# A gather in steps of 8 slots from a table written by runs, and expert outputs gated by matmuls with diagonal gates

## The reference, cut to what matters

```
h = x @ W_gat                                   # 4096 nodes x (4 heads x 4 experts)
a_src, a_dst = (h*att_src).sum, (h*att_dst).sum # one number for a node and head
e = leaky_relu(a_src[src] + a_dst[dst], 0.2)    # for 524288 edges and each node's loop
alpha = softmax of e over the edges of one dst
agg = segment_sum(h[src] * alpha, dst) + b_gat
scores = layernorm(agg, gamma, beta).mean over heads      # 4096 x 4 experts
top 2 of the 4 scores, w = softmax of these two, 0 for the other two
out = sum over experts of w[e] * (gelu(x @ W1[e] + b1[e]) @ W2[e] + b2[e])
```

## Time and profile before

| | |
|---|---|
| median of 3 runs | 1105.31 us (1095.95 to 1108.36) |
| the profiled execution | 1085.32 us |
| its span, first to last instruction | 1083.6 us |
| mean granted clock of TensorE | 0.852 of full |
| busy: PE, DVE, ACT, POOL | 765.5, 661.9, 349.7, 204.3 us |
| last normalisation ends, features begin | about 806 us |
| first and last indirect DMA issued | 845.3 and 972.7 us |
| gates known, first gate transposition | 1025.6 us |
| last addition of outputs ends | 1075.6 us |

### The profile page before, as it was taken

The page is one execution under the profiler, slowest core; times in us unless marked ns, Lnnn a source line. Parts: engine busy times, 40 slices in busy tenths (PEclk is TensorE's granted clock), DMA queues, the critical chain, the costliest instruction groups (busy, mean ns, idle before and its releaser), DMA issues.

```text
span 1083.6 us, 13898 instructions
## 1 busy us (share of the span) xinstructions
PE 765.5 (71%) x4268; PEld 467.3 (43%) x4308; DVE 661.9 (61%) x1367; ACT 349.7 (32%) x519; POOL 204.3 (19%) x200
## 2 busy tenths in 40 slices
PE   4369920108989989989987787899489999203753
PEld 1212210107878878878842332544155433002332
DVE  3599778755656646646658677594663233226754
ACT  4421130004544535545532333510024566103500
POOL 5180010000000000000040000100000677770055
PEclk9588965558999999999999899999787999655866
DMA  8000000010000000000000000000017000110001
GB/s 304 0 1 1 1 0 0 2 77 3 2 1 0 0 0 0 0 0 0 0 1 1 0 0 0 2 1 1 2 42 15 8 8 7 8 8 2 1 20 58
DMA packets 19866, 15.60 MB, mean 14 GB/s; under 512 B 14016, under 2 KB 17728, under 8 KB 19440
## 3 DMA queue, kind: packets, MB, share of 16 engines
q1 hardware_dynamic: 16512, 13.93, 5.2%
q0 software_dynamic: 3312, 1.16, 1.6%
HBM read 10.43 MB, written 4.65 MB: 14 GB/s over the span
## 4 chain that ended last, share of the span: by engine, by line
DVE 16%; PE 15%; issue 10%; POOL 8%; DMA 3%; DVEq 1%; ACT 1%; POOLq 0%; PEld 0%; PEldq 0%; SPq 0%
PE banks L1516 12%; POOL rows_g L576 7%; DVE kept L1208 2%; DVE wide_buf L1168 1%; DMA rows_g<-table_d,g_idx 1%; PE banks L1881 1%; PE banks L1797 1%; DVE wide_buf L1174 1%; POOL wide_buf L592 1%; DVE tie L1172 1%; DVE kept L1267 1%; DMA table_d<-shared 1%; DVE T L846 1%; DVE round_k L1266 1%; PE banks L1549 1%
## 5 line engine op out<-in xcount | busy, mean ns | idle before, releaser
L1117 DVE TENSOR_TENSOR wide_buf<-banks,small 128x1024 f32<-128x1024 f32 x72 | 88.1, 1224 | 118.3 <-ACT small L713 118.3
L1516 PE MATMUL banks<-wide_buf 128*128 128x256 f32 (+1 forms) x720 | 145.7, 350 | 0.0
L1516 PEld LDWEIGHTS banks<-wide_buf 128*128 128x128 f32 x720 | 123.1, 195 | 12.9
L576 POOL DMA_INDIRECT rows_g<-table_d,g_idx x96 | 99.4, 1035 | 125.8 <-DVEq L1426 96.9
L1516 PE MATMUL banks<-XP 128*128 128x32 bf16 (+1 forms) x1168 | 95.2, 222 | 27.4 <-DVE XP L971 27.4
L1516 PE MATMUL banks<-taps_w,small 128*128 128x128 f32 x618 | 92.2, 296 | 20.5 <-issue 20.5
L1516 PEld LDWEIGHTS banks<-taps_w,small 128*128 128x128 f32 x618 | 85.2, 202 | 30.9 <-issue 21.1
L711 ACT ACTIVATE small<-banks,neg_x 128x512 f32<-128x512 f32 x72 | 49.5, 688 | 151.6 <-remote 64.7
L1516 PEld LDWEIGHTS banks<-XP 128*128 128x128 bf16 (+1 forms) x1168 | 60.1, 107 | 61.7 <-issue 32.4
L727 ACT COPY wide_buf<-banks 128x512 f32<-128x512 f32 (+1 forms) x87 | 49.6, 570 | 95.8 <-PE banks L1516 95.1
L971 DVE TENSOR_TENSOR XP<-lo_b,XP 128x2048 bf16<-128x2048 bf16 x64 | 77.8, 1215 | 0.0
(11 more groups left out here) (314 smaller groups left out, 1168.1 us busy)
## 6 DMA issues: line engine op xcount, KB each, us to landing
wide_buf<-in_edges SPq DMA_DIRECT2D x2, 1536.0 KB, 15.3
generic_d<-generic SPq DMA_DIRECT2D x1, 2064.0 KB, 7.3
X<-in_x SPq DMA_DIRECT2D x4, 512.0 KB, 5.0
out_x<-X SPq DMA_DIRECT2D x4, 512.0 KB, 2.6
rows_g<-table_d,g_idx POOLq DMA_INDIRECT x96, 2.4
wide_buf<-in_edges SPq DMA_DIRECT2D x2, 512.0 KB, 9.8
XP<-in_m_w SPq DMA_DIRECT2D x2, 512.0 KB, 4.5
taps_w<-in_w_dcn SPq DMA_DIRECT2D x1, 576.0 KB, 16.7
```

The lines of the kernel that those rows point to most:

```text
L576: pool.indirect_dma_start(rows_g[:, half, k, :], None, table_d, bass.IndirectOffsetOnAxis(ap=g_idx[:, c:c + 1], axis=0)).then_inc(rows_lan ...
L1117: nc.vector.tensor_tensor(near_w[s % RING], banks[:, 0:2, :], hat_x[:, h:h + 1, :].to_broadcast([P, 2, CHUNK]), ALU.mult).then_inc(w_done, 1)
L1516: return nc.tensor.matmul(o, l, r, start=start, stop=stop, **kw)
```

## The change

The change has three parts.

The gather runs in steps of 8 slots (`STEP`), two halves of 4, and so many steps as the fullest partition needs (`N_STEPS`, from the same counts). The one-hot work of a step stands between the waits for its two halves, it is half as large, and it reads `bucket_dst` without the copy `per_hi`. POOL is released right behind the computation of a_dst, and the large comparison of `slot_keys` becomes `slot_ends`, called after L1421. `table_d` is written with each partition's 32 rows as one run ("(p t) f"), and the slots' indices are computed to match, in two more instructions.

The scoring chain is shortened: gamma and beta are folded into `gat_g` and `gat_b` ahead of time, and gamma's product and the sum over heads stand ahead of the wait for the square root.

The experts' outputs become pixel-major: `expert_out` takes the hidden values as the stationary operand, 128 pixels at a time, 8 matmuls of 128 columns in place of 2 of 512, and ACT only copies. Gating is done by PE: for each chunk one matmul of 512 columns adds the gated biases (`m_b2` tiled over the partitions, times `gate_rows`, which POOL makes from the transposed gates), and 16 matmuls of 128 columns multiply a block of `y_exp` with a diagonal matrix of one expert's gates for 128 pixels, all summed in one bank. DVE makes 12 diagonals of a chunk in one instruction of 128x1536, ACT the other 4. DVE adds the bank to X.

```diff
-            sp.dma_start(table_d.rearrange("(t p) f -> p t f", p=P), table[:, :, :]).then_inc(table_out, 16)
+            sp.dma_start(table_d.rearrange("(p t) f -> p t f", p=P), table[:, :, :]).then_inc(table_out, 16)
             sp.wait_ge(adst_ready, 1)
-            sp.dma_start(table_d_dst.rearrange("(t p) h -> p t h", p=P), a_dst[:, :, :]).then_inc(adst_out, 16)
+            sp.dma_start(table_d_dst.rearrange("(t p) h -> p t h", p=P), a_dst[:, :, :]).then_inc(adst_in, 16)
...
+            nc.gpsimd.memset(own_tiles[:, :], 1.0).then_inc(sel_made, 1)
+            for base, step in ((0, -EXPERTS), (EXPERTS - 1, EXPERTS)):
+                pool.wait_ge(sel_made, 11 if base == 0 else 12)
+                nc.gpsimd.affine_select(out=own_tiles[:, :], in_=own_tiles[:, :], compare_op=ALU.is_ge, fill=0.0, base=base,
+                                        pattern=[[step, HIS]], channel_multiplier=1 if base == 0 else -1).then_inc(sel_made, 1)
...
-                    for k in range(HALFR):
-                        c = half * HALFR + k
-                        pool.indirect_dma_start(rows_g[:, half, k, :], None, table_d,
-                                                bass.IndirectOffsetOnAxis(ap=g_idx[:, c:c + 1], axis=0)).then_inc(rows_landed[half][k // GROUP], 16)
-
-            with pool.Fori(0, ways) as r:
+                    for k in range(HALF_STEP):
+                        c = half * HALF_STEP + k
+                        pool.indirect_dma_start(rows_step[:, half, k, :], None, table_d,
+                                                bass.IndirectOffsetOnAxis(ap=g_idx[:, c:c + 1], axis=0)).then_inc(rows_landed[half][k // 2], 16)
+
+            with pool.Fori(0, steps) as r:
...
-            with pool.Fori(0, CHUNKS) as i:
-                pool.wait_ge(gated, EXPERTS * (i + 1) + 2)
-                pool.sem_inc(passed, 1)
-                for e in (0, 2):
-                    nc.gpsimd.tensor_tensor(y_exp[e][:, bass.ds(i, 1), :], y_exp[e][:, bass.ds(i, 1), :],
-                                            y_exp[e + 1][:, bass.ds(i, 1), :], ALU.add).then_inc(gated_b, 1)
-                pool.wait_ge(gated_b, 3 * i + 2)
-                pool.sem_inc(passed, 1)
-                nc.gpsimd.tensor_tensor(y_exp[0][:, bass.ds(i, 1), :], y_exp[0][:, bass.ds(i, 1), :],
-                                        y_exp[2][:, bass.ds(i, 1), :], ALU.add).then_inc(gated_b, 1)
+            pool.wait_ge(gates_known, 3)
+            pool.wait_ge(sel_made, 13)
+            for i in range(CHUNKS):
+                if i >= 2:
+                    pool.wait_ge(gated, i - 1)
+                nc.gpsimd.tensor_tensor(gate_rows[i % 2], gate_t.unsqueeze(1).to_broadcast([P, CHUNK // P, P]),
+                                        own_tiles[:, 4 * i:4 * i + 4].unsqueeze(2).to_broadcast([P, CHUNK // P, P]), ALU.mult).then_inc(rows_gated, 1)
...
-                nc.scalar.activation(y_exp[e][:, i, :], ps[4 + e % 2][:, :], ACT.Identity, bias=m_b2[:, e:e + 1]).then_inc(my_done, 1)
+                nc.scalar.copy(y_exp[e][:, i, :], ps[4 + e % 2][:, :]).then_inc(my_done, 1)
...
+            act.wait_ge(gates_known, 2)
+            nc.scalar.copy(gate_t, ps[0][:, 0:P]).then_inc(gates_known, 1)
+            for i in range(CHUNKS):
+                if i >= 2:
+                    act.wait_ge(gated, i - 1)
+                for e in range(EXPERTS):
+                    last = nc.scalar.activation(gate_diag[i % 2][:, 3, e, :], ident[:, :], ACT.Copy, scale=gate[:, 4 * i + 3, e:e + 1])
+                last.then_inc(diag_act, 1)
...
+                steps_ = num[:, N_STEPS:N_STEPS + 1]
+                run(nc.vector.tensor_scalar(steps_, counts_max[:, 0:1], float(STEP - 1), None, ALU.add))
+                run(nc.vector.tensor_scalar(steps_, steps_, 3, None, ALU.logical_shift_right))
...
-                step(nc.vector.tensor_scalar(slot_idx[:, 0:P], slot_int, LAST, None, ALU.bitwise_and))
+                step(nc.vector.tensor_scalar(slot_lo, slot_int, P - 1, 5, ALU.bitwise_and, ALU.logical_shift_left))
+                step(nc.vector.tensor_scalar(slot_idx[:, 0:P], slot_int, 7, HIS - 1, ALU.arith_shift_right, ALU.bitwise_and))
+                step(nc.vector.tensor_tensor(slot_idx[:, 0:P], slot_idx[:, 0:P], slot_lo, ALU.add))
...
+            def slot_step(R, r):
+
+                g = R * STEPS + r
+                step, n = chained(m1_chain, g * SLOT_STEP, True)
+
+                def rows_in(half):
+                    at = r * STEP + half * HALF_STEP
                     for landed in rows_landed[half]:
-                        dve.wait_ge(landed, g * (16 * GROUP) + 16 * GROUP)
+                        dve.wait_ge(landed, g * (16 * 2) + 16 * 2)
                         dve.sem_inc(passed, 1)
-                    step(nc.vector.tensor_copy(g_idx[:, half * HALFR:(half + 1) * HALFR], slot_idx[:, bass.ds(at + ROUND, HALFR)]))
+                    step(nc.vector.tensor_copy(g_idx[:, half * HALF_STEP:(half + 1) * HALF_STEP], slot_idx[:, bass.ds(at + STEP, HALF_STEP)]))
                     dve.sem_inc(idx1_ready, 1)
-                    step(nc.vector.tensor_copy(feat_s[:, :, bass.ds(at, HALFR)], rows_g[:, half, :, 0:HE].rearrange("p k f -> p f k")))
-                    step(nc.vector.tensor_tensor(z_by_head[:, :, bass.ds(at, HALFR)], z_by_head[:, :, bass.ds(at, HALFR)],
-                                                 rows_g[:, half, :, HE:ROW].rearrange("p k h -> p h k"), ALU.add))
+                    step(nc.vector.tensor_copy(feat_s[:, :, bass.ds(at, HALF_STEP)], rows_step[:, half, :, 0:HE].rearrange("p k f -> p f k")))
+
+                def logits_in(half):
+                    cols = bass.ds(r * STEP + half * HALF_STEP, HALF_STEP)
+                    step(nc.vector.tensor_tensor(z_by_head[:, :, cols], z_by_head[:, :, cols],
+                                                 rows_step[:, half, :, HE:ROW].rearrange("p k h -> p h k"), ALU.add))
                     dve.sem_inc(max1_done, 1)
-                assert n[0] == SLOT_ROUND
+
+                rows_in(0)
+                step(nc.vector.tensor_tensor(oh_slots, his[:, bass.ds(r * STEP, STEP)].unsqueeze(2).to_broadcast([P, STEP, HIS]),
+                                             lane[:, 0:HIS].unsqueeze(1).to_broadcast([P, STEP, HIS]), ALU.is_equal))
+                step(nc.vector.tensor_tensor(pick_grid, oh_slots.unsqueeze(2).to_broadcast([P, STEP, HEADS, HIS]),
+                                             bucket_dst[:, :, :].rearrange("p t h -> p h t").unsqueeze(1).to_broadcast([P, STEP, HEADS, HIS]), ALU.mult))
+                step(nc.vector.tensor_reduce(z_by_head[:, :, bass.ds(r * STEP, STEP)].rearrange("p h k -> p k h"), pick_grid, AX_X, ALU.add))
+                logits_in(0)
+                rows_in(1)
+                logits_in(1)
+                assert n[0] == SLOT_STEP
...
+            dve.sem_inc(max1_done, 2)
...
-            dve.wait_ge(adst_in, 16)
-            run(nc.vector.tensor_copy(per_hi[:, :, :], bucket_dst[:, :, :].rearrange("p t h -> p h t")))
-            dve.sem_inc(max1_done, 2)
-            ways = dve.value_load(num[0:1, N_WAYS:N_WAYS + 1], min_val=1, max_val=WAYS)
+            slot_ends()
+            dve.wait_ge(adst_in, 32)
+            steps = dve.value_load(num[0:1, N_STEPS:N_STEPS + 1], min_val=1, max_val=STEPS)
             rest = dve.value_load(num[0:1, N_REST:N_REST + 1], min_val=0, max_val=MAX_ROUNDS // WAYS - 1)
-            with dve.Fori(0, ways) as r:
-                slot_round(0, r)
+            with dve.Fori(0, steps) as r:
+                slot_step(0, r)
...
-            run(nc.vector.tensor_scalar(stat[:, 0, :], stat[:, 0, :], 1.0 / HE, None, ALU.mult))
-            run(nc.vector.tensor_tensor(prod[:, :, :], prod[:, :, :], wide(0), ALU.subtract))
+            run(nc.vector.scalar_tensor_tensor(prod[:, :, :], wide(0), -1.0 / HE, prod[:, :, :], ALU.mult, ALU.add))
             run(nc.vector.tensor_tensor(agg, prod[:, :, :], prod[:, :, :], ALU.mult))
             run(nc.vector.tensor_reduce(stat[:, 1, :], agg, AX_X, ALU.add))
-            run(nc.vector.tensor_scalar(stat[:, 1, :], stat[:, 1, :], 1.0 / HE, None, ALU.mult))
             dve.sem_inc(f_ask, 1)
+            run(nc.vector.tensor_tensor(prod[:, :, :], prod[:, :, :], gat_g[:, :].unsqueeze(1).to_broadcast([P, HIS, HE]), ALU.mult))
+            run(nc.vector.tensor_reduce(score[:, :, :], prod[:, :, :].rearrange("p t (h e) -> p t e h", h=HEADS), AX_X, ALU.add))
             dve.wait_ge(f_exp, 2)
             run(nc.vector.reciprocal(stat[:, 1, :], stat[:, 1, :]))
-            run(nc.vector.tensor_tensor(prod[:, :, :], prod[:, :, :], wide(1), ALU.mult))
-            run(nc.vector.tensor_tensor(prod[:, :, :], prod[:, :, :], row(1), ALU.mult))
-            run(nc.vector.tensor_tensor(prod[:, :, :], prod[:, :, :], row(2), ALU.add))
-
-            run(nc.vector.tensor_reduce(score[:, :, :], prod[:, :, :].rearrange("p t (h e) -> p t e h", h=HEADS), AX_X, ALU.add))
```

(54 more changed lines are left out.)

94 lines of the change are left out of this document (39 added, 55 removed).

## The result

The changed kernel takes 1071.23 us (median of 4 runs, 1068.46 to 1072.75), the kernel before 1100.63 (4 runs, 1095.3 to 1108.36): ratio 0.9725, 95% interval 0.965 to 0.9799. The forecast was 1079, with a range of 1060 to 1098. The profiled executions show less: spans of 1083.6 and 1071.0 us, so 12.6 us, where the sum gave 26. Later runs of both, beside each other, took that side: 1083.63 against 1071.15. The total was met, and by luck; its parts were not, and this is what the rest is about.

A forecast was written before the change was run, and what follows sets the result against it. Behind the last normalisation it took three stretches to carry the change: the gather's start, its length (POOL's issue sets the pace) and gating. +1.2 - 15 - 11 gave -26 from 1085.3, about 1059; plus 20 for the median, 1079 (range 1060 to 1098).

The forecast's parts named there:

- The total: Whole kernel: 26 us less, about 1059 us for a profiled execution, 1079 us for the median of runs.
- Counts: Counts before the rounds: four more dependent DVE operations on the path to the last normalisation, +1.2 us.
- Start of the gather: Table write 2.5 us, first gather about 825, 20 us earlier; `last_row` lands about 831, DVE takes first rows about 839.3.
- Length of the gather: 88 gathers in 11 steps, 11.3 us a step, set by the handshake; last rows answered at 961.4, -15 us.
- Rival C: The gather gives nothing: 12.5 us instead of 11.3, or 12 steps; +12 to +14 us, 1092; chance 0.13.
- The bound of 10.0 a step: Lower bound for a gather step, by POOL's issue alone: 8 x 1.25 us, giving -28 us.
- The experts: Experts beside the gather: smaller matmuls add 1.7 us for 28 experts, end near 928, covered by the gather.
- Scores: Scoring chain on DVE after the gather: shorter, gates known 2.1 us earlier.
- Gating: Last stage, on PE: 4.4 us a chunk, last addition over at 1064.8 against 1075.58; -11 us including the scoring chain's 2.1.
- rival D: PE pairs run at the low clock through gating: 71 us instead of 35, 1114 us; chance 0.06.
- rival B: POOL's configuration for gating is loaded behind the wait: +7 us, 1086 us; chance 0.17.
- The tail: The store behind the last addition: taken to stay as it was, no gain.

The follow-up runs named there:

- a0_again: The changed kernel, unchanged, run again beside runs of the kernel before on the same chip: 1071.15 us, ratio 0.989.
- a_ends: The changed kernel with only the 4.4 us comparison for the segment ends moved into the wait for the last row: 1066.56 us, ratio 0.9837.
- a_perhi: The changed kernel with the a_dst rows copied once to a contiguous tile, which the one-hot product reads instead of the strided operand: 1063.04 us, ratio 0.9807.
- a_first: The changed kernel with a step's one-hot compare, product and reduce ahead of the wait for its first rows: 1053.27 us, ratio 0.9714.
- a_best: The changed kernel with contiguous operand, one-hot work ahead of the first wait, and the segment-ends comparison in the wait for the last row: 1040.40 us, ratio 0.9602.
- b3_written: The kernel before with POOL's loop of the last stage written out eight times, with constant waits and addresses: 1084.04 us, ratio 1.000.
- b0_again: The kernel before, unchanged, profiled once more: 1086.04 us.
- b1_table: The kernel before with only the table part: table written by runs, indices to match, buffer credits given right after the table: 1070.28 us, ratio 0.9861.
- a_step16: The changed kernel with steps of 16 slots instead of 8, so 96 gathers instead of 88: 1060.22 us, ratio 0.9773.
- b2_gate: The kernel before with the gating part alone: pixel-major expert outputs, diagonal gates, products accumulated in PSUM: 1072.86 us, ratio 0.9892.

## Why the prediction was right in the total and wrong in its parts

- **Counts** (+1.2): features start 1.3 us later (807.73 against 806.40). Right, as far as this can be read: over the kept traces the start lies between 804.54 and 807.88 with the old counts and between 805.75 and 809.43 with the new, so one pair of profiles can't show 1.2 us.
- **Start of the gather**: table write 2.2 us (2.5 forecast), first gather 825.76 (825). `last_row` was forecast to land at 831; DVE goes on at 835.35. I had priced the a_dst write and the read behind it at 6 to 7 us by subtraction, 15.1 less the table's 8.98, as if the two writes had simply added. They had overlapped: without the table's, from the a_dst issue at 824.01 to DVE at 835.35, write and read still take 11.3, and in a0_again that write alone lands after 11.6. This and the 0.4 us more until the loop put DVE's first rows at 843.98 instead of 839.3. a_ends shows that a delay here reaches the end: the 4.4 us moved gave 4.6.
- **Length of the gather**, the step that failed: "the period of a step is ... 11.3 us". It is 12.8. The form was right (3 x 1.25, landing, DVE's work, POOL's answer), and in the step shown above three terms were larger. DVE's work takes 5.44 us against 4.7, by the product alone: 1.98 instead of 1.22 us (I took its length from the contiguous one of the kernel before, and the change drops just that copy; a_perhi gives 0.8 back). POOL's way from release to first gather takes 0.94 us against 0.3. The first half lands 2.66 us behind its last issue (892.47) against 2.5. Together 3.75 + 2.66 + 5.44 + 0.94 = 12.8. The gaps on DVE, 1.1 us, were no larger than the 1.2 forecast. The second step starts 6.0 us late (850.29 against 844.3), the nine steps to the last one take 116.2 us instead of 103.7: 18.5 us, and -15 became +3.4. Rival C came true in size (12.5 in its text), but not for its reason: landing reaches 3.0 to 3.65 us only in the last three steps, and the rest is the product and POOL's answer.
- **The bound of 10.0 a step** was reachable: the one-hot work could stand ahead of the wait. a_first and a_best show 10.7 and 10.0. I had seen that the work lies between landing and release, and didn't ask what moving it would give.
- **The experts** (+1.7, hidden): 15.33 a chunk against 15.16, 1.2 us in all, hidden. Right in a0_again, where the last copies end before the table load at 926.74 (928 forecast); in the changed kernel's first profile they ended at 977.1, with the gaps told above, and the time was the same.
- **Scores** (-2.1): -1.7. Right.
- **Gating** (-9 of the 11): chunks 4.43 us apart (4.4 forecast), PE at the high clock from the second chunk on (windows below), so rival D falls; POOL not late, so rival B falls. The size is right, -9.3. The new stage was counted from its own parts, and these came out; which part of the old one goes was left open, and it isn't the one that a reader would take from the change. Between two chunks the diagonals save only 0.28 us; 7.4 us come ahead of the first add, where the kernel before waited for POOL's configuration. I had that row and used it for a rival only, not as the main part of the gain. That the load is what went is read from the two traces; b3_written shows only that unrolling doesn't remove it.
  The windows of the changed kernel (us, busy time and count of PE, PEld, DVE, ACT, POOL, granted clock, DMA):

```profile
1031.00:1036.00 5.00, 5.00 (x33) 5.00 (x32) 0.40 (x1) 0.00 (x0) 1.30 (x1) 0.66 0.00 0
1036.00:1051.00 15.00, 15.00 (x114) 13.09 (x113) 9.53 (x8) 5.14 (x16) 4.16 (x4) 1.00 0.09 36
1051.00:1067.00 16.00, 16.00 (x129) 14.57 (x127) 7.34 (x6) 2.57 (x8) 2.08 (x2) 1.00 0.17 67
```

- **The tail** ("The store behind it stays"): 5.0 us less, not forecast; a term put at nothing. Every kernel with the old gating (before, b0_again, b1_table, b3_written) ends 8.0 us behind its last add, those with the new one 3.0, and the last store lands in 2.6 us in all. What ends last in the old ones is POOL's drain: 9.66 to 9.79 us long in these four traces, begun with POOL's last addition. In all kernels with the new gating it takes 8.9 to 9.6 us, but POOL is through two chunks earlier, and it is over before the last store has landed. b3_written, which only unrolls POOL's loop, leaves POOL's last addition where it was and the tail at 8.0.
- **The total** was met by luck: the sum said -26, the two kernels side by side on one chip give -12.5. I added the 20 us between profile and median to the forecast, and those 20 us were not the kernel's: by the later runs the forecast of 1059 for a profiled execution missed by 14, while 1079 lies 8 from 1071. A gain taken 13.5 us too large and a start taken 20 us too high nearly cancelled.

## What to carry to other kernels

When a double-buffered loop is cut into smaller steps, the time between landing and release does not shrink with them: list what the consumer does between the two, and move ahead of the wait all that doesn't need the data. Whether fewer, larger steps or more, smaller ones win depends on that list first (the same pair of sizes differed by 10.9 us one way and 6.6 the other), then on the first pause and on how long an operation beside the transfers holds them. Test the parts of a change one by one: here two parts of -14.7 and -12.7 made -12.5 together.

## What the runs showed of the hardware

- An indirect DMA issued by POOL takes 0.94 us, but one that starts while DVE multiplies two operands ends 0.8 us behind that product: 4.33 us beside a product of 3.89 (a_step16), 2.17 beside 1.98, 2.14 beside 2.29 in the kernel before, 1.40 beside 1.23 in a_perhi. One that starts just ahead of the product keeps its 0.94 us (a_best, 876.84). The Trainium skill, "SBUF — State Buffer", section "SBUF: two separate sides", describes a port pair that DVE and POOL share as an exclusive lock: of a DVE operation with two inputs in SBUF and a POOL operation that reads SBUF, the one that starts first holds it for its whole length and the other waits. The traces agree in who waits and until when; that an indirect DMA counts as such a POOL operation, no run here shows.
- The stride of an operand that repeats by broadcast costs each time it is read: 2.02 against 1.22 us for 128x1024, 3.89 against 2.29 for 128x2048; one copy of 0.28 us ahead of the loop saves it.
- POOL's configuration for another kind of operation took 5.9 us (L560) and 6.8 to 7.5 us (the last additions) where it was issued behind the wait, and cost nothing where it was issued ahead of it (L547, b2_gate, the changed kernel).
- POOL's drain at the end of the program takes 8.9 to 9.8 us in all traces. It was hidden where POOL's last operation began 9.5 us before the last add's end, and it made 5.0 us of the time where POOL worked to the end.
